# Attention with experts on one core: two buffers for the widened probabilities, and the product with the values one unit earlier

## The reference, cut to what matters

```python
# x: (4, 512, 512), context: (4, 512, 512); 16 heads of 32
xn = layernorm(x)
q = (xn @ Wq + bq) * 32 ** -0.5              # 2048 queries
k, v = (ctx @ Wkv + bkv)                     # 2048 keys
q, k, v = fq_sym(q), fq_sym(k), fq_sym(v)    # rounded to 8 bits, with a scale
attn = softmax(q @ k.T)                      # 16 heads, 2048 x 2048 each
attn = fq_unsigned(attn)                     # rounded to 0..255 per row, with a scale
x = x + (attn @ v) @ Wp + bp
h = layernorm(x)
# router: the top 4 of 32 experts for each token, weights normalised
# each expert: silu(clip(h @ wg.T)) * clip(h @ wu.T) @ wd.T; and one shared expert
return x + sum(prob[e] * expert[e](h) for e in top4) + shared(h)
```

## Time and profile before

| | |
|---|---|
| median of 3 runs | 1447.6 us |
| lowest and highest | 1443.19 and 1450.12 us |
| profiled execution | 1445.22 us |
| its span, first to last instruction | 1443.5 us |
| mean granted TensorE clock | 0.982 |
| PE busy | 1272.0 us (88%) |
| PE weight loads | 633.2 us (44%) |
| DVE busy | 978.0 us (68%) |
| ACT busy | 799.7 us (55%) |
| POOL busy | 876.3 us (61%) |

### The profile page before, as it was taken

How to read it: one execution, slowest core, us unless ns; L and a number is a source line. 1 busy time by engine, 2 the same in 40 slices (tenths; PEclk the granted TensorE clock), 3 DMA queues, 4 the chain that set the end, 5 groups by cost and what they waited for, 6 DMA issues and landing times.

```text
span 1443.5 us, 28685 instructions
## 1 busy us (share of the span) xinstructions
PE 1272.0 (88%) x7890; PEld 633.2 (44%) x7891; DVE 978.0 (68%) x1886; ACT 799.7 (55%) x1030; POOL 876.3 (61%) x894
## 2 busy tenths in 40 slices
PE   8999478888888888888887879999999999999995
PEld 3444134444444444444443434444444444444442
DVE  4667799999999999999999646823333333333332
ACT  2233599989999999999999743222122222222221
POOL 3213388899999999999899812143444444344443
PEclk9999799999999999999999899999999999999998
DMA  7655876776676666776777956465678776685442
GB/s 250 146 139 124 168 122 139 140 143 141 137 150 136 142 137 138 145 145 131 147 142 135 184 204 174 101 164 113 165 184 217 204 196 162 155 223 139 85 76 31
DMA packets 398568, 215.53 MB, mean 149 GB/s; under 512 B 356903, under 2 KB 357031, under 8 KB 398514
## 3 DMA queue, kind: packets, MB, share of 16 engines
q1 hardware_dynamic: 378338, 176.05, 51.8%
q0 software_dynamic: 20176, 38.83, 14.9%
HBM read 100.28 MB, written 37.49 MB: 95 GB/s over the span
## 4 chain that ended last, share of the span: by engine, by line
PE 40%; issue 20%; DVE 17%; DMA 9%; POOL 6%; ACT 5%; DVEq 1%; SPq 1%; POOLq 1%; ACTq 0%
PE psS L813 18%; DMA out_y<-mem 7%; PE psS L821 7%; DVE mem L593 6%; DVE mem L577 6%; POOL mem L667 4%; ACT mem L534 4%; PE psS L1664 3%; PE psS L448 3%; PE psT L1278 1%; PE psAV L1651 1%; PE psP L805 1%; DMA mem<-mem 1%; POOL mem L650 1%; DVE mem L1076 1%
## 5 line engine op out<-in xcount | busy, mean ns | idle before, releaser
L534 ACT ACTIVATE mem<-mem 128x2048 uint8<-128x2048 f32 x256 | 534.3, 2088 | 46.1 <-POOL mem L650 44.2
L667 POOL TENSOR_SCALAR mem<-mem 128x2048 bf16<-128x2048 uint8 x256 | 486.6, 1901 | 26.4 <-DMA mem<-mem 6.2
L448 PE MATMUL psS<-mem 128*128 128x512 bf16 x1024 | 312.8, 388 | 114.3 <-DVE mem L577 50.1
L813 PE MATMUL psS<-mem 128*128 (+1 forms) x752 | 349.0, 606 | 0.1
L593 DVE TENSOR_SCALAR_CACHE_REDUCE mem<-psS,mem 128x1024 f32<-128x1024 f32 x256 | 327.5, 1279 | 0.8 <-PE psS L448 0.7
L577 DVE TENSOR_SCALAR_CACHE_REDUCE mem<-psS 128x1024 f32<-128x1024 f32 x256 | 312.4, 1220 | 17.8 <-PE psS L448 16.0
L847 DVE TENSOR_SCALAR mem<-psS 128x512 f32<-128x512 f32 x94 | 64.9, 691 | 319.6 <-PE psS L813 314.3
L841 ACT ACTIVATE mem<-mem 128x256 f32<-128x256 f32 x94 | 39.2, 416 | 354.5 <-DVE mem L847 354.5
L1210 POOL DMA_INDIRECT out_y<-mem x78 | 124.0, 1590 | 143.7 <-DMA out_y<-mem 129.5
L813 PEld LDWEIGHTS psS<-mem 128*128 128x128 f32 x752 | 136.3, 191 | 147.4 <-issue 144.2
L821 PE MATMUL psS<-mem 128*128 (+1 forms) x376 | 178.4, 596 | 2.0 <-ACT mem L835 2.0
(11 more groups left out here) (210 smaller groups left out, 1173.1 us busy)
## 6 DMA issues: line engine op xcount, KB each, us to landing
mem<-in_moe_w SPq DMA_DIRECT2D x64, 768.0 KB, 5.8
mem<-xn_dram SPq DMA_DIRECT2D x32, 256.0 KB, 3.0
xn_dram<-mem SPq DMA_DIRECT2D x29, 256.0 KB, 2.1
mem<-in_x SPq DMA_DIRECT2D x28, 256.0 KB, 2.9
mem<-mem SPq DMA_TRANSPOSE x292, 3.1
mem<-in_ctx_in SPq DMA_DIRECT2D x16, 256.0 KB, 3.6
out_y<-mem SPq DMA_DIRECT2D x16, 256.0 KB, 2.2
mem<-in_wkv SPq DMA_DIRECT2D x2, 1024.0 KB, 7.1
```

The lines of the kernel that those rows point to most:

```text
L448: last = nc.tensor.matmul(psS[c][:, k * D:(k + 1) * D], qT[pm][:, hm, :], kT[:, hm, c * HALF + k * D:c * HALF + (k + 1) * D], start=True, ...
L534: nc.scalar.activation(p8[slot], S[slot], ACT.Exp, bias=NB[:, slot:slot + 1], scale=sq[p][:, h:h + 1], accum_out=Z[p][:, h:h + 1]).then_in ...
L667: nc.gpsimd.tensor_scalar(pb[slot], pT[slot].bitcast(U8).rearrange("p (j q b) -> p j b q", b=2, q=P), 1.0, 0.0, ALU.mult, ALU.add).then_in ...
L813: last = nc.tensor.matmul(bankG[o], xT[o if xo is None else xo][:, c, :], w(c * 2 * I, 2 * I), start=(c == 0), stop=(c == DC - 1))
```

## The change

Two constants and what hangs on them. LAG goes from 7 to 6: PE takes the product of unit n - 6 in step n, and the division on DVE, which stands at h = LAG, moves with it. A new constant WIDE = 2 is the number of places of `pb`: the widening of unit m writes place m mod 2 and waits until the product of unit m - 2 is done, where it waited for that of m - 4. The words of the two places are left unused, so nothing else moves in memory.

```diff
-    LAG = 7
+    LAG = 6
...
     NS = 4
+    WIDE = 2
...
-        pb = [cut(TK // 2, BF16).rearrange("p (j b q) -> p j b q", b=2, q=P) for _ in range(NS)]
+        pb = [cut(TK // 2, BF16).rearrange("p (j b q) -> p j b q", b=2, q=P) for _ in range(WIDE)]
+        at[0] += (NS - WIDE) * TK // 2
...
-                ho, slot, bank = (h - LAG) % H, (l - LAG) % NS, psAV[p if h >= LAG else 1 - p]
+                ho, slot, bank = (h - LAG) % H, (l - LAG) % WIDE, psAV[p if h >= LAG else 1 - p]
...
-                if due(m - NS + 1):
-                    pool.wait_ge(av_done, m - NS + 1)
-                    apart(pool, m - NS + 1)
+                if due(m - WIDE + 1):
+                    pool.wait_ge(av_done, m - WIDE + 1)
+                    apart(pool, m - WIDE + 1)
...
-                    pb[slot], pT[slot].bitcast(U8).rearrange("p (j q b) -> p j b q", b=2, q=P),
+                    pb[slot % WIDE], pT[slot].bitcast(U8).rearrange("p (j q b) -> p j b q", b=2, q=P),
```

## The result

| | before | after |
|---|---|---|
| median | 1448.86 us (4 runs) | 1494.13 us (4 runs) |
| lowest and highest | 1443.19 and 1450.26 us | 1491.94 and 1495.47 us |
| ratio, 95% interval | | 1.0316 [1.0294, 1.0337] |
| profiled execution, its span | 1445.22 and 1443.5 us | 1494.69 and 1493.0 us |
| mean granted TensorE clock | 0.982 | 0.968 |

The change costs 45.3 us. The forecast was 27.5 us more (1475), with 1492 at the top of the range: the sign was right, the time lies 2 us above the range.

A forecast was written before the change was run, and what follows sets the result against it. DVE was taken as the bound, POOL close behind; the change closes a two-unit loop over DVE, POOL and PE without slack. 24.6 (tiles) + 0.5 (first units) + 2.4 (end) = 27.5 us more, forecast 1475 us, range 1459 to 1492.

The forecast's parts named there:

- The two buffers at nothing in the steps: POOL's widening waits for the product of m - 2, always over by then behind a shift: costed at nothing.
- Rival D: The two buffers bind: the wait for `av_done` holds POOL in every unit, time above 1490 us; chance 0.02.
- 2.4 us at the end: End of attention: shared expert's first matmuls start some 2.4 us later, delaying last transposes, router and experts; bounds 0 to 4.
- Shift of 2 to 4: POOL, two units with its own work (root, normalised tokens) at h = 2 and 3: 6.94 us.
- shift of 4 to copy of 6: From POOL's shift through widening, product and scores to DVE's copy two units on: 3.39 us; DVE loses 1.43 us.
- to the shift 0.09: Loop piece from the end of the copy's maximum on DVE to the shift on POOL: 0.09 us, in a 4.76 us loop.
- the rest unexplained: Copy of 14 to its shift: 1.37 us by pieces, 1.59 seen; the forecast took the middle, 1.48.
- crossing from 11 to 14: Copy of 11 through POOL and PE, over projection and router, to the copy of 14: 8.02 us; DVE alone took 7.59.
- rival B: PE stands more, so its clock drops for a stretch in every tile: 7 us in all, 1482 us; chance 0.10.
- Copies of 6 to 10: DVE's stretch from the copy of unit 6 to that of 10, with the queries' scale: 11.03 us a tile.
- Rival C: Loop longer throughout, 5.14 us, with 0.61 for the product and 0.31 copy to shift: 45 us, 1492 us; chance 0.12.
- Rival A: Not slower: DVE's copies stay the bound and PE's new wait at h = 4 to 6 is swallowed, 1447.6 us; chance 0.08.

The follow-up runs named there:

- its control: The kernel before (seven units, four buffers) with only its loop over pairs of tiles written out: 1444.54 us, ratio 0.9969.
- written_out: The change with all sixteen tiles written out, no loop over pairs, so waits are against constants: 1471.85 us, ratio 1.0193.
- after: The change itself, LAG 6 and two places, against the kernel before: 1494.13 us, ratio 1.0316.
- order_of_waits: The change with POOL's two waits ahead of the shift swapped, exponential first and then the copy: 1481.38 us, ratio 1.0222.
- fill: The change with matmuls that nobody reads added on PE at h = 15, 0, 1 and 2: 1485.6 us, ratio 1.0249.

## Why the prediction was right and wrong

**The bound and the mechanism: right.** The path leaves DVE and runs through POOL and PE; the time comes from waits, not from work. The two edits apart and the written-out loop against its control show it.

**The two buffers at nothing in the steps: right.** The places cost nothing in the tiles (527.18 against 527.20). Rival D, places that bind in every unit, is out.

**2.4 us at the end: the size came out, partly by luck.** Against the copy of unit 252 the transposes moved by 2.07 us (25.84 - 23.77). The forecast had them follow from the shared expert's first matmuls, which it put 2.4 us later; these moved by 1.60 us (from 12.25 to 13.85 us behind that copy). With the lag alone they moved by 1.33, and the transposes still came 0.65 earlier. It is the last widening's wait, which two places bring, that costs 2.7 to 2.9 us, and the shorter lag gives back 0.7.

**Shift of 2 to 4, shift of 4 to copy of 6: right,** 6.93 and 3.43 us against 6.94 and 3.39.

**The step that failed is "to the shift 0.09".** The value came from the earlier trace rows, in the first tile, which is written out and has no counting behind its waits. In the loop it is 0.31, and the trace of before had that too: from the end of unit 14's maximum (488.60) to the shift (488.91). The prediction met it at unit 14, called it "the rest unexplained", took the middle there and left 0.09 everywhere else. One round of the loop is therefore 4.76 + 0.22 = 4.98 by the forecast's pieces, and was 4.94. Two rounds are 9.88 us, longer than POOL's own 9.53 from shift of 14 to shift of 2, so the circle sets that stretch, not POOL. The same 0.22 lies in the crossing from 11 to 14 and behind the copy of 14. Of the 1.21 us a tile above forecast, 0.35 (9.88 - 9.53), 0.16 and 0.11 are put down to this: 0.62, half of it.

**The clock, rival B,** was given 0.10 as an alternative, but it came on top: 0.27 us a tile, half of the 0.5 that it was priced at. "34.80 of 42.74 are still 81%" was the wrong evidence, a mean over the tile; PE stands at its waits in one stretch of it, and there the clock fell. The Trainium skill, TensorE: Matmul & The Clock Gate, section A second HAM failure mode: psum-queue depth-cycling, says that small idle times between groups of matmuls can make the clock swing. The traces agree in this: it fell and rose again in 6 of 12 tiles behind waits of 0.8 us, and with the same stretch filled it stood at 0.99 or 1.00 in all 12.

**Copies of 6 to 10: 0.21 us too short.** In the stretch from 487.33 two copies start at the end of the reading of the maximum before (488.62 and 495.30), 0.08 us later than when they start with it; this was not taken further.

Together 0.62 + 0.27 + 0.21 = 1.10 of the 1.21 us. Against the kernel before, whose mean tile is 41.05 and not 40.98, a tile rose by 1.12 us more than forecast (2.88 - 1.76); times 14 that is 15.7 of the 17.8 us by which the rise was missed. The rest lies outside these tiles: from the first second-half copy to that of unit 32 the two profiled executions took 80.41 and 82.97 us, 2.56 more where 0.5 were forecast.

**Rival C** had the mechanism and nearly the time (1492), but its pieces were wrong: it added 0.61 for the product, which was 0.41 to 0.42 (468.80 to 469.21, 483.20 to 483.62), and no clock. **Rival A** is out: it gave a sum of zero, since DVE gets no more to do, and the share of the time that DVE is busy fell while the time rose.

## What to carry to other kernels

Before a consumer is moved nearer to its producer, follow the waits round until they close a circle, add up its pieces and compare with the number of units that it spans times the time of one; an engine at 98% does not hide a circle with no slack. Take each piece from the place where it will count: the wait of a written-out first tile isn't that of the loop, and a difference of 0.22 us that looks like noise in one row counts once in every crossing. Look there too for what the program puts between the wait and the work, as the counting here. An average of busy time over a tile says nothing of the clock in the one stretch where the engine stands.

## What the runs showed of the hardware

- From the end of a producer's instruction on DVE to the start of its consumer on POOL: 0.10 us with waits against constants (`written_out`), 0.31 us in the loop, where two waits against registers, each with an instruction that counts, stand between (`after`), 0.21 us with one of them moved ahead (`order_of_waits`). Which part of such a wait costs the 0.1 us was not tried.
- With PE standing 0.79 us twice in a row, the granted clock was 0.51 in the 3 us behind, where a busy tile before stood at 1.00; a half of scores went from 0.59 to 1.02 us. It fell in that stretch in 6 of 12 tiles, in 2 of 12 where PE stood 0.70 us twice (`order_of_waits`), and in none where it stood 0.59 us (`written_out`) or was filled (`fill`), though there it fell just behind the stretch in two and in three tiles. Why the other 6 are spared, with the same waits, stays open.
